# The half-swapped copy of k in the rotary attention stage: made by four partition-shifted ScalarE copies of one bank of transposes

## The reference

```python
h  = _rmsnorm(hidden_states, ln1_w)
kv = _rmsnorm(kv_states, ln1_w)
q = (h @ Wq).reshape(bsz, q_len, 16, 64).transpose(0, 2, 1, 3)
k = (kv @ Wk).reshape(bsz, k_len, 4, 64).transpose(0, 2, 1, 3)
v = (kv @ Wv).reshape(bsz, k_len, 4, 64).transpose(0, 2, 1, 3)
q = q * cos + rotate_half(q) * sin
k = k * cos + rotate_half(k) * sin      # rotate_half swaps the halves of 32 of each head of 64
k, v = repeat(k, 4), repeat(v, 4)
probs = softmax(q @ k^T / 8 + attention_mask)
hidden = residual + (probs @ v) @ Wo
x = _rmsnorm(hidden, ln2_w)
return hidden + (silu(x @ Wgate) * (x @ Wup)) @ Wdown
```

## Time and profile before

| what | value |
|---|---|
| time, median of 3 runs (lowest, highest) | 571.61 us (570.94, 571.62) |
| the profiled execution's own time | 567.52 us |
| its span, first to last instruction | 565.7 us |
| busy: TensorE matmul, weight load | 474.9 us (84%), 376.2 us (66%) |
| busy: VectorE, ScalarE, GpSimd | 366.4 us (65%), 305.9 us (54%), 262.6 us (46%) |
| mean granted TensorE clock | 0.967 of 2.4 GHz |

### The profile page before, as it was taken

The page is one execution under the profiler, slowest core; times in us unless marked ns, Lnnn a source line. Parts: engine busy times, 40 slices in busy tenths (PEclk is TensorE's granted clock), DMA queues, the critical chain, the costliest instruction groups (busy, mean ns, idle before and its releaser), DMA issues.

```text
span 565.7 us, 17230 instructions
## 1 busy us (share of the span) xinstructions
PE 474.9 (84%) x7014; PEld 376.2 (66%) x7014; DVE 366.4 (65%) x929; ACT 305.9 (54%) x738; POOL 262.6 (46%) x319
## 2 busy tenths in 40 slices
PE   2899899999999987885578778788888978897885
PEld 1577677777777765775456657576676757676664
DVE  5777756776877752256559695776858666674522
ACT  1488677777777773475344454525635344433431
POOL 5567765797787777689303231213212132111100
PEclk9999999999999996999689899999999989999989
DMA  8940000000000000000000000000000000000000
GB/s 291 219 150 2 3 2 3 3 3 3 2 3 3 3 2 0 1 2 1 0 1 3 2 2 1 2 2 12 1 10 2 1 13 1 12 1 12 10 1 20
DMA packets 12278, 11.43 MB, mean 20 GB/s; under 512 B 5160, under 2 KB 10152, under 8 KB 12200
## 3 DMA queue, kind: packets, MB, share of 16 engines
q1 hardware_dynamic: 11624, 9.01, 6.2%
q10 hardware_dynamic: 576, 1.32, 0.6%
HBM read 9.29 MB, written 1.05 MB: 18 GB/s over the span
## 4 chain that ended last, share of the span: by engine, by line
PE 56%; DVE 19%; issue 9%; POOL 8%; ACT 7%; DMA 1%; POOLq 0%; ACTq 0%; DVEq 0%
PE ps L442 6%; PE ps L682 5%; PE ps L599 4%; PE ps L456 4%; PE ps L621 4%; DVE wide L1242 4%; PE ps L432 4%; PE ps L424 3%; PE ps L629 2%; PE ps L671 2%; DVE mx L1306 2%; PE ps L541 2%; PE ps L583 2%; DVE p L1308 2%; POOL yg L1431 2%
## 5 line engine op out<-in xcount | busy, mean ns | idle before, releaser
L1486 POOL TENSOR_TENSOR probs<-p,rc 128x512 f32<-128x512 f32 x32 | 33.5, 1048 | 167.8 <-DVE rc L1317 167.8
L933 ACT ACTIVATE p<-p 128x512 f32<-128x512 f32 x32 | 20.2, 630 | 119.6 <-DVE p L1308 119.5
L1089 DVE TENSOR_REDUCE negm<-ps 128x8 bf16<-128x512 f32 x96 | 59.5, 682 | 26.3 <-PE ps L424 26.3
L791 ACT ACTIVATE shared<-ps 128x512 f32<-128x512 f32 x96 | 57.0, 600 | 21.2 <-PE ps L442 19.5
L1446 POOL TENSOR_TENSOR wide<-wide,cv 128x1024 f32<-128x1024 f32 x24 | 45.5, 1896 | 30.0 <-DVE wide L1068 30.0
L442 PE MATMUL ps<-cst,p 128*128 128x128 f32 x384 | 58.7, 276 | 0.4 <-ACT shared L791 0.4
L785 ACT ACTIVATE p<-ps 128x512 f32<-128x512 f32 x96 | 54.5, 596 | 3.7 <-PE ps L432 3.7
L442 PEld LDWEIGHTS ps<-cst,p 128*128 128x128 f32 x384 | 45.2, 141 | 16.1 <-issue 8.8
L1373 POOL TENSOR_TENSOR rstd<-veps,neghalf 128x2 f32<-128x2 f32 x40 | 29.2, 730 | 55.4 <-DVE veps L1113 36.6
L1306 DVE TENSOR_REDUCE mx<-ps 128x8 f32<-128x512 f32 x32 | 21.9, 686 | 30.6 <-PE ps L682 30.6
L583 PE MATMUL ps<-shared,wq 128*128 128x256 f32 x128 | 34.2, 402 | 7.7 <-DVE wide L1242 7.7
(11 more groups left out here) (182 smaller groups left out, 1150.1 us busy)
## 6 DMA issues: line engine op xcount, KB each, us to landing
late<-in_mask_l SPq DMA_DIRECT2D x2, 512.0 KB, 11.6
result<-x_all SPq DMA_DIRECT2D x8, 128.0 KB, 1.8
x_all<-in_x_tok SPq DMA_DIRECT2D x1, 768.0 KB, 7.4
wide<-in_ctx_t SPq DMA_DIRECT2D x1, 768.0 KB, 9.0
rv<-in_rv ACTq DMA_DIRECT2D x1, 768.0 KB, 7.4
wa<-in_wa SPq DMA_DIRECT2D x1, 512.0 KB, 10.0
w<-in_w SPq DMA_DIRECT2D x2, 256.0 KB, 6.8
wq<-in_wq SPq DMA_DIRECT2D x1, 512.0 KB, 7.4
```

Of the source, the lines that this page charges most:

```text
L791: A_(pt[:, w % 2, r, :], ring_of("p", w, r), ACT.Copy).then_inc(sm["act_pt"], 1)
L1089: V.tensor_reduce(negm[:, n % 4, :], ps[:, S_BANK[r], :].rearrange("p (a k) -> p a k", k=S), AX.X, ALU.max, negate=True).then_inc(sm["dve_ ...
```

## The change

`kcs`, its two additions and the use `ks` go. ScalarE reads the bank of the use `kt` five times: once whole, as before, to k3[c=0], and then four times 32 partitions, each to the neighbouring block of 32 in k3[c=1] (block i comes from block i^1). This is the same swap of halves, made along the partitions. Since `ks` stood in the tables, the ring and the positions in step 3 shift with it, and `scores3` waits for `kt` alone.

```diff
         STEPS = (
...
-            (("ks", 1), ("q2", 1), ("q3", 1), ("mg1", -2), ("mu1", -2), ("out", -1)),
+            (("q2", 1), ("q3", 1), ("mg1", -2), ("mu1", -2), ("out", -1)),
...
-        BY_ACT = ("in", "l_in", "l_text", "l_gate", "l_back", "kt", "ks", "v", "m_in")
+        BY_ACT = ("in", "l_in", "l_text", "l_gate", "l_back", "kt", "v", "m_in")
...
-                    src = [(kc if what == "kt" else kcs)[:, i, a * 128:a * 128 + 128] for a in range(2) for i in range(TG)]
+                elif what == "kt":
+                    pe.wait_ge(sm["d_kr"], g + 1)
+                    src = [kc[:, i, a * 128:a * 128 + 128] for a in range(2) for i in range(TG)]
...
                     pe.wait_ge(*released("q3", g))
-                    pe.wait_ge(*released("ks", g))
+                    pe.wait_ge(*released("kt", g))
...
-                elif what in ("kt", "ks"):
-                    ins = A_(k3[:, gs, ("kt", "ks").index(what), :, :].rearrange("p a k -> p (a k)"), bank, ACT.Copy)
+                elif what == "kt":
+                    A_(k3[:, gs, 0, :, :].rearrange("p a k -> p (a k)"), bank, ACT.Copy)
+                    for i in range(4):
+                        to, by = slice(32 * i, 32 * i + 32), slice(32 * (i ^ 1), 32 * (i ^ 1) + 32)
+                        ins = A_(k3[to, gs, 1, :, :].rearrange("p a k -> p (a k)"), bank[by, :], ACT.Copy)
...
             def sum_k(g):
                 dve.wait_ge(*released("k", g))
-                half = HD3 // 2
...
-                for j in range(2):
-                    V.tensor_tensor(kcs.rearrange("p t (n d) -> p (t n) d", d=HD3)[:, :, j * half:j * half + half],
-                                    swapped(kc[:, :, :], j), swapped(ks, j), ALU.add).then_inc(sm["d_ks"], 1)
-                dve.wait_ge(sm["d_ks"], 2 * g + 2)
                 V.tensor_tensor(kc[:, :, :], kc[:, :, :], ks[:, :, :], ALU.add).then_inc(sm["d_kr"], 1)
```

More of the change, by code:

```diff
@@ L94, in build @@
         k3 = wide[:, 4096:6144].rearrange("p (g c a k) -> p g c a k", g=2, c=2, a=2)
-        kcs = wide[:, 6144:6656].rearrange("p (t n) -> p t n", t=TG)
         xn_all = wide[:, 0:NT * D].rearrange("p (n d) -> p n d", d=D)
@@ L229, in build @@
             g_st g_mv g_ve g_r g_yn g_yg g_x
-            h_sq h_ms h_r h_n p_use d_use a_use d_kr d_ks s3 s3m s3x s3e s3s s3r s3n t3 t3e pv3 pv3e
+            h_sq h_ms h_r h_n p_use d_use a_use d_kr s3 s3m s3x s3e s3s s3r s3n t3 t3e pv3 pv3e
             m_sq m_ms m_r m_n m_th st_out""".split()
@@ L563, in part_in @@
                     src = [hm[:, g % 2, i, :] for i in range(TG)]
-                elif what in ("kt", "ks"):
-                    if what == "kt":
-                        pe.wait_ge(sm["d_kr"], g + 1)
-                    else:
-                        pe.wait_ge(sm["d_ks"], 2 * g + 2)
-                    src = [(kc if what == "kt" else kcs)[:, i, a * 128:a * 128 + 128] for a in range(2) for i in range(TG)]
+                elif what == "kt":
+                    pe.wait_ge(sm["d_kr"], g + 1)
+                    src = [kc[:, i, a * 128:a * 128 + 128] for a in range(2) for i in range(TG)]
                 elif what == "l_in":
@@ L640, in fill @@
                     pe.wait_ge(sm["f_y"], NG)
-                if what in ("in", "m_in", "kt", "ks", "l_in", "l_back"):
+                if what in ("in", "m_in", "kt", "l_in", "l_back"):
                     ins = part_in(what, g)
@@ L1260, in sum_k @@
                 dve.wait_ge(*released("k", g))
-                half = HD3 // 2
-                def swapped(a, j):
-                    return a.rearrange("p t (n d) -> p (t n) d", d=HD3)[:, :, (1 - j) * half:(2 - j) * half]
-                for j in range(2):
-                    V.tensor_tensor(kcs.rearrange("p t (n d) -> p (t n) d", d=HD3)[:, :, j * half:j * half + half],
-                                    swapped(kc[:, :, :], j), swapped(ks, j), ALU.add).then_inc(sm["d_ks"], 1)
-                dve.wait_ge(sm["d_ks"], 2 * g + 2)
                 V.tensor_tensor(kc[:, :, :], kc[:, :, :], ks[:, :, :], ALU.add).then_inc(sm["d_kr"], 1)
```

## The result

| | before | changed |
|---|---|---|
| time, median (lowest, highest), 4 executions each | 571.28 us (568.98, 571.62) | 585.42 us (580.96, 587.19) |
| ratio to before, 95% interval | | 1.0245 (1.0179 to 1.0311) |
| the profiled execution: time, span | 567.52, 565.7 us | 587.19, 585.3 us |
| busy TensorE, VectorE, ScalarE | 474.9, 366.4, 305.9 us | 487.8, 361.4, 321.9 us |
| mean granted TensorE clock | 0.967 | 0.933 |

The kernel is about 2.5% slower; 571.0 was predicted, with 574.0 as the upper end. Run again it took 578.63 us against 569.92, ratio 1.0196 (1.0105 to 1.0287), so the loss is some 9 to 14 us. TensorE has less to do and is busy 13 us longer: that is the first sign.

What follows compares the result with a forecast made beforehand. VectorE's and TensorE's work looked dear, ScalarE's cheap; ms's 1.27 us slack decided. Rounds 0.2 - 1.4 + 0.0 + 1.3 - 0.7 = -0.6 us gave 566.9 profiled, 571.0 against the timed median; range 567.8 to 574.0.

Steps and rivals of the forecast that it cites:

- Price of the copies: End of step 2 on ScalarE: four added copies at 0.485 us each, 1.94 us, between 0.48 and 2.40.
- no overlap: Upper bound for the ScalarE copies: each takes the whole 0.60 us of the kt copy, 2.40 for four.
- dear copies: Rival: ScalarE copies that read one bank do not overlap, sum +2.2 us, 573.8 us; chance 0.10.
- Who waits: Behind the copies: the four squares, hence ms, then VectorE's readings of q2 and q3, mu1, out and next scores.
- Rounds 2 to 4 at 0.0: Last stage: ms 0.7 us late, out starting at 407.8 against 407.82 in round 3, 0.0 in each round.
- the room that the prediction counted as 0.77: Step 3 ahead of out: the two ks items that left gave 0.77 us, which the ms wait eats.
- one stretch fewer: Rival: the shift carries the chain past one lower-clock stretch, -1.5 us more, 569.5 us; chance 0.10.
- a slower clock: Rival: longer TensorE waits directly before scores or out bring lower-clock stretches; one more gives 572.5 us, two 574.0; chance 0.16.
- Round 0, +0.2: Sums end at 310.73 against an ms at 310.56; VectorE's 0.80 us gained is given back: +0.2 us.
- Round 1, -1.4: ms 1.15 us late, out early without the ks copy, scores waiting for q3's reading alone at 342.5: -1.4 us.
- Rounds 5 and 6: Round 5: ms 1.9 us late, out +1.3 us. Round 6: no squares or ms, out -0.7 us.
- The moved sum at no cost: Step 3: the sum over the batch before, now behind mg1's reading, comes later but costs nothing.

Runs made afterwards that it cites:

- f1: Changed kernel with other kt copies by group (four unshifted of 32 partitions, four of 128, two of 64, four of 128x128), swap left out: 576.09 us.
- g1: Changed kernel with four ScalarE copies of 128 partitions x 512 in place of the four of 32 partitions, swap left out: 581.63 us, ratio 1.0204.
- e4: Changed kernel with TensorE computing mg1 three times for all groups, and v three times from group 2 on: 579.62 us, ratio 1.0183.
- g2: Changed kernel with three ScalarE copies of 128 partitions x 512 in place of the four of 32 partitions, swap left out: 569.87 us, ratio 0.9985.

## Why the prediction was wrong, point by point

- **Price of the copies.** Wrong: 0.60 us from start to start, not 0.485, and the squares put off by 2.53 us, not 1.94. That is a little beyond the bound "no overlap" and the rival "dear copies" (2.40, which gave 573.8), since the first copy and the first square do not overlap their forerunners either. That rival's reason, several readings of one bank, fell in f1. That width is not what costs came out, though no row before showed it: four copies of 32 partitions take four times the length of a whole one. The Trainium skill ("ScalarE: Activation LUTs", section "What ACT_TABLE_LOAD costs") has two parts to it: 186 + 0.833 x 512, an estimate of some 612 ns for one, and 93 ns less back to back. By the rows the second holds for copies of 128 partitions (0.48) and not for the narrow ones behind each other (0.60). In rounds the dearer price is worth 231.6 - 228.2 = 3.4 us (changed kernel against g1).
- **Who waits.** Right: ms waits for the sums of squares, 1.20 to 1.22 us in rounds 2 to 4, and 2.48 and 2.49 in rounds 1 and 5. mg1 is early, and TensorE waits ahead of mu1 for VectorE's L1241.
- **Rounds 2 to 4 at 0.0.** Wrong, 8.7 us in all. For round 3 (+3.6): ms 1.20 late; the way from ms to out is 0.9 us shorter at full speed (the room that the prediction counted as 0.77); so 0.3 late at out. Then 0.95 for mu1 at the lower clock (2.08 - 1.13), 0.66 for out (0.11 of it even at full speed, 3.84 against 3.73), and 1.68 ahead of ms (28.66 us into the round instead of 25.78, less the wait of 1.20), above all for the scores of step 2, which ran at the lower clock behind the wait for a_tok (397.54: masks of 0.63 instead of 0.38). 0.3 of 3.6 is waiting, some 3.2 is clock. Measured another way, e4 puts it at 0.7 and 2.8. The rival "one stretch fewer" did not come either: the first scores of round 1 still run at the lower clock (3.11 us; 3.62 before).
- **The rival "a slower clock".** The mechanism was right, even its place ("directly followed by the scores or out"). Its size and its chance were not. I priced it as one or two stretches of 1.5 us in the whole stage, since the only long wait that I set against it (1.99 us, then out at 3.84) had kept its speed. It comes in nearly every round. The step that failed is there, and in the 0.0 of rounds 2 to 4 that follows from it: I kept the sum of the waits and did not see that two of 1.3 us would become one of 2.7, so the lower clock behind it stood at nothing in these rounds. g1, with the copies at my own price, has rounds of 228.2 us in sum against 218.8 before, where my sum has 0.6 less than before, and takes 581.6 us in all.
- **Round 0, +0.2.** Measured +3.4. TensorE waits 4.72 us ahead of this round's scores instead of 1.32 and runs them at the lower clock; VectorE waits 1.51 us at ms, and TensorE 5.54 ahead of the next scores instead of 3.06. The second fence has the scores before:

```profile
289.34 0.61 PE L667 MATMUL ps<-m3a,idb 128*128 128x512 bf16 x1 [4.72 <-DVE wide L1241]
...
291.15 3.69 PE L678 MATMUL ps<-wide 64*64 64x64 f32 x128
...
314.21 0.17 DVE L1228 TENSOR_SCALAR ms<-ss 128x4 f32<-128x4 f32 x1 [1.51 <-ACT sq L865]
...
318.02 0.61 PE L667 MATMUL ps<-m3a,idb 128*128 128x512 bf16 x1 [5.54 <-DVE wide L1241]
```

```profile
289.09 0.39 PE L671 MATMUL ps<-m3a,idb 128*128 128x512 bf16 x1 [1.32 <-DVE wide L1242]
...
290.05 2.10 PE L682 MATMUL ps<-wide 64*64 64x64 f32 x128
```

The round's own scores begin 1.81 us behind its first mask instead of 0.96 and take 3.69 us instead of 2.10: 2.4 us of the 3.4 are this clock, and some 0.6 the dearer copies. The prediction saw the wait coming ("the wait ahead of the scores grows"), but only ahead of round 1's scores, and did not put the clock behind it in the sum.
- **Round 1, -1.4.** Measured -0.1. ms comes 25.3 us into the round instead of 23.2, so 2.1 late where 1.15 was put down: 0.6 for the dearer copies, and of VectorE's gain of 0.80 only 0.46 reached ScalarE. out starts early as predicted, though by less, 24.2 us into the round instead of 25.9. Behind 1.66 us of wait it runs at the lower clock (5.44 instead of 3.84), but that is the smaller part here:

```profile
342.24 5.44 PE L595 MATMUL ps<-wo,late 128*128 128x128 f32 x32 [1.66 <-ACT late L945]
...
343.28 0.17 DVE L1228 TENSOR_SCALAR ms<-ss 128x4 f32<-128x4 f32 x1 [2.48 <-ACT sq L865]
...
344.69 2.35 DVE L1241 TENSOR_TENSOR wide<-ps,cst 128x1024 f32<-128x1024 f32 x2
...
347.51 0.38 PE L667 MATMUL ps<-m3a,idb 128*128 128x512 bf16 x1
```

The reading of q3 ends at 347.04 and the next scores start at 347.51. With out at full speed they would still wait for that reading, so the clock costs 0.4 to 0.5 us of this round, and the late ms the rest.

- **Rounds 5 and 6.** Measured +1.3 and -0.6 for +1.3 and -0.7. In round 5 out ran at full speed (3.84), so the sum of waits was all there was. That ms was 1.9 us later into the round, as said, is luck: the squares are put off by 2.53 us instead of 1.94, and the copy of kt comes 0.65 us earlier into the round, which the sum had at nothing. Run again, the round is +1.5. In round 6 there are no squares.
- **The moved sum at no cost.** Right within what can be told: back in its old place, rounds 3 and 4 do not get shorter.

## What to carry to other kernels

Put work behind which another engine's wait hangs ahead of work that nobody waits for: here four squares ahead of four copies took away a loss of 2 to 2.5%. When a change takes work from TensorE, don't only add up its waits, but ask whether two short ones become one long one, and what stands right behind it; price that at the lower clock in every repetition of the loop. Price a form of instruction that no row shows at its full length, without overlap, and ask whether the slack behind it bears that.

## What was not expected of the hardware

- ScalarE copies of 512 elements from PSUM stand 0.48 us apart with 128 partitions, from the same bank too. Block by block, with 32 or 64 partitions each, they stand 0.60 apart, with or without a shift; but a first block that begins where the whole copy ahead began stands 0.48 behind it (f1), a shifted one 0.61. Moving the blocks to other partitions costs nothing over leaving them in place, beyond that first start.
- In this kernel the step is steep: with TensorE's wait ahead of mu1 at 1.58 us (g2), one of four runs of out was at the lower clock, with 2.07 us (g1) all four; the time goes from 569.9 to 581.6 us for 0.5 us more on ScalarE.
- With idle matmuls in the wait ahead of mu1, out is at the higher clock behind it (3.84 us in eight of eight), and the seven rounds sum to some 4.5 us less, e4's long round 6 included. In the total that is not clear: the ratios are 1.0183 (e4) and 1.0135 (f3) against 1.0196, and the intervals overlap.
- Open: whether it is the changed first partition that keeps narrow copies from overlapping, and why the same wait (2.68 us in round 5, 2.4 us ahead of a_tok) is followed by full speed in one round and not in another.
